# One layer of attention and matmul in float32: steps in batches of two, and softmax denominators summed straight into the heads' rows

## What is computed

```python
q = x @ wq.T + bq;  k = x @ wk.T + bk;  v = x @ wv.T + bv
scores = einsum('bqhd,bkd->bhqk', q, k) / sqrt(32), causal
attn = softmax(scores) @ v
x1 = layernorm(x + attn @ wo.T + bo)
s_x = 448 / max|x1|;  s_w = 448 / max|w|
y = clip(x1 * s_x, -448, 448) @ clip(w * s_w, -448, 448) / (s_x * s_w)
out = layernorm(x1 + y)
```

## Time and profile before

| | us |
|---|---|
| median of 3 runs | 2793.57 |
| lowest, highest | 2790.87, 2796.37 |
| profiled execution, its own time | 2800.54 |
| its span, first to last instruction | 2798.8 |
| PE, DVE, ACT, POOL busy | 2545.9, 1731.8, 1298.5, 728.2 |
| mean granted clock of TensorE | 0.944 of full |

### The profile page before, as it was taken

How to read it: one execution, slowest core, us unless ns; L and a number is a source line. 1 busy time by engine, 2 the same in 40 slices (tenths; PEclk the granted TensorE clock), 3 DMA queues, 4 the chain that set the end, 5 groups by cost and what they waited for, 6 DMA issues and landing times.

```text
span 2798.8 us, 36168 instructions
## 1 busy us (share of the span) xinstructions
PE 2545.9 (91%) x14312; PEld 1553.7 (56%) x14312; DVE 1731.8 (62%) x1293; ACT 1298.5 (46%) x1412; POOL 728.2 (26%) x442
## 2 busy tenths in 40 slices
PE   7999998999999889999989999899999897599998
PEld 5888884344444444444444444444444445488887
DVE  6343438977766666666667767666667764344444
ACT  1222225765665555565655666556656552100000
POOL 2321301221111212121221221212121212466663
PEclk9999998999999999999989999999999999799999
DMA  7343343521221112121121221112121110322221
GB/s 233 114 164 120 114 139 110 125 61 39 50 58 39 39 46 50 39 58 39 39 46 39 50 58 39 40 45 50 39 58 39 39 42 23 128 90 90 90 89 61
DMA packets 150742, 198.01 MB, mean 71 GB/s; under 512 B 8558, under 2 KB 108878, under 8 KB 148558
## 3 DMA queue, kind: packets, MB, share of 16 engines
q1 hardware_dynamic: 126990, 144.71, 19.9%
q10 hardware_dynamic: 23616, 51.39, 4.8%
HBM read 123.72 MB, written 72.35 MB: 70 GB/s over the span
## 4 chain that ended last, share of the span: by engine, by line
PE 80%; DVE 6%; POOL 5%; issue 4%; ACT 2%; DMA 1%; SPq 0%; POOLq 0%; ACTq 0%; DVEq 0%
PE bank L1146 17%; PE bank L1158 17%; PE bank L1131 15%; PE bank L1043 13%; PE bank L1208 13%; POOL moments L521 2%; POOL moments L519 2%; PE bank L1176 2%; ACT prob L697 2%; PE bank L1168 2%; DVE acc L930 2%; DVE stats L751 1%; PE bank L1128 1%; PE bank L1197 1%; DVE res L909 1%
## 5 line engine op out<-in xcount | busy, mean ns | idle before, releaser
L697 ACT ACTIVATE prob<-bank 128x1024 f32<-128x1024 f32 x1088 | 1054.0, 1021 | 554.0 <-PE bank L1146 553.1
L930 DVE TENSOR_TENSOR acc<-acc,prob 128x2048 f32<-128x2048 f32 x420 | 965.0, 2298 | 286.7 <-ACT prob L697 273.8
L1146 PE MATMUL bank<-q_st,keys 98*128 98x512 f32 x2176 | 662.3, 422 | 171.0 <-ACT prob L697 159.4
L1146 PEld LDWEIGHTS bank<-q_st,keys 98*128 98x128 f32 x2176 | 399.5, 196 | 416.5 <-ACT prob L697 325.4
L1158 PE MATMUL bank<-prob,v_t 128*32 128x512 f32 x4352 | 605.1, 629 | 6.6 <-issue 3.4
L568 POOL TENSOR_SCALAR_AFFINE_SELECT prob<-prob 128x1024 f32<-128x1024 f32 x128 | 159.3, 1269 | 996.3 <-ACT prob L697 996.3
L926 DVE TENSOR_TENSOR acc<-prob 128x2048 f32<-128x2048 f32 x60 | 137.5, 2292 | 184.6 <-ACT prob L697 175.8
L1043 PE MATMUL bank<-xt_hi,w_hi 128*128 128x512 f32 x576 | 228.4, 397 | 16.4 <-DVE xt_lo L772 15.7
L1043 PE MATMUL bank<-xt_hi,w_lo 128*128 128x512 f32 x576 | 227.1, 394 | 0.0
L1043 PE MATMUL bank<-xt_lo,w_hi 128*128 128x512 f32 x576 | 226.9, 394 | 0.0
L1131 PE MATMUL bank<-wo_hi,att_lo 128*128 128x512 f32 x512 | 218.6, 427 | 0.0
(11 more groups left out here) (109 smaller groups left out, 2540.8 us busy)
## 6 DMA issues: line engine op xcount, KB each, us to landing
q_st<-q_hi_d SPq DMA_DIRECT2D x128, 256.0 KB
xt_raw<-x_t SPq DMA_DIRECT2D x16, 1024.0 KB, 6.9
q_hi_d<-part_hi ACTq DMA_DIRECT2D x64, 256.0 KB, 2.1
q_lo_d<-part_lo ACTq DMA_DIRECT2D x64, 256.0 KB, 2.3
q_st<-q_lo_d SPq DMA_DIRECT2D x64, 256.0 KB
res<-x SPq DMA_DIRECT2D x32, 512.0 KB, 6.1
x_d<-res SPq DMA_DIRECT2D x32, 512.0 KB, 2.6
x<-x_d SPq DMA_DIRECT2D x32, 512.0 KB, 3.2
```

The costliest lines, as they stand in the source:

```text
L697: nc.scalar.activation(prob[:, s % SLOTS, 2 * p:2 * p + 2], bank[:, 2 * p:2 * p + 2], ACT.Exp, scale=SCALE).then_inc(p_done, 1)
L930: nc.vector.tensor_tensor(acc[:, n % 2], acc[:, n % 2], new, ALU.add).then_inc(acc_done, 1)
L1146: last = nc.tensor.matmul(bank[:, g].rearrange("p (a n) -> p a n", n=P), keys[:, k // QT, k % QT * P:(k % QT + 1) * P], queries[:, :, g], ...
```

## The change

It does five things.

- PE's loop goes by batches `u` of two steps: `scores(2u)`, then `between(u)` (denominators and fillers), `scores(2u+1)`, `weigh_values(2u-2)`, `weigh_values(2u-1)`.
- The denominators are summed by 4 matmuls of 128x512 with a 32-column weight of ones, each into its head's 32 rows. The 4 spreading matmuls of each group are gone.
- VectorE inverts 128x512 instead of 128x128, and multiplies by `r_den` in SBUF instead of a bank in PSUM.
- `places` has new numbers and a tenth name: DEVIATION, where GpSimd does its three small instructions. For the first tile of most pairs: SPLIT 4, HALF0 6 to 12, SUM0 12, HALF1 14 to 20, SUM1 20, DEVIATION 22, SCALE_ROW 27, LARGEST 28.
- The semaphore `ln1` is counted by the moments alone; two new ones, `scaled` and `measured`, count L716 and L951.

```diff
         for n in range(len(groups)):
-            at = begins[n] + lengths[n] + 1
-            den_at.append(max(at, den_at[-1] + 4) if n else at)
+            at = (begins[n] + lengths[n] + 2) // 2
+            den_at.append(max(at, den_at[-1] + 2) if n else at)
...
             if p < len(pairs) - 2:
-                names = (21, 24, 29, 30, 32, 37, 38, 40, 42) if second else (4, 7, 12, 13, 15, 20, 21, 23, 25)
+                names = (21, 24, 30, 30, 32, 38, 38, 39, 44, 45) if second else (4, 6, 12, 12, 14, 20, 20, 22, 27, 28)
...
-        SPLIT, HALF0, HALF0_END, SUM0, HALF1, HALF1_END, SUM1, SCALE_ROW, LARGEST = range(9)
+        SPLIT, HALF0, HALF0_END, SUM0, HALF1, HALF1_END, SUM1, DEVIATION, SCALE_ROW, LARGEST = range(10)
...
-                for place in range(first, last + 1):
-                    fillers.setdefault(place, []).append((q, half, place - first, last - first + 1))
+                for place in range(first // 2, last // 2 + 1):
+                    fillers.setdefault(place, []).append((q, half, place - first // 2, (last - first) // 2 + 1))
...
-                if s in sum1_at:
-                    q = sum1_at[s]
+                if s in deviation_at:
+                    q = deviation_at[s]
                     inverse_deviation(moments[:, q % 2], ln1, q * LN)
                     shift_of(moments[:, q % 2], ln1, q * LN)
...
-                if s - 2 in group_of_end:
-                    n = group_of_end[s - 2]
+                for n in moved_at.get(s, []):
...
-                nc.vector.reciprocal(r_den[:], bank[:, DEN_BANK, 0:P]).then_inc(den_read, 1)
+                nc.vector.reciprocal(r_den[:], bank[:, DEN_BANK]).then_inc(den_read, 1)
...
-                dve.wait_ge(spread_done, n + 1)
+                dve.wait_ge(den_read, n + 1)
                 dve.wait_ge(pv_moved, n + 3)
-                nc.vector.tensor_tensor(attended(n), attended(n), bank[:, DEN_BANK], ALU.mult).then_inc(att_ready, 1)
+                nc.vector.tensor_tensor(attended(n), attended(n), r_den[:], ALU.mult).then_inc(att_ready, 1)
...
-                if s - 1 in group_of_den:
-                    invert(group_of_den[s - 1])
-                if s - 3 in group_of_den:
-                    normalise_group(group_of_den[s - 3])
+                if s % 2 == 0 and s // 2 in group_of_den:
+                    invert(group_of_den[s // 2])
+                if s % 2 == 1 and s // 2 in group_of_den:
+                    normalise_group(group_of_den[s // 2])
...
                 for g in range(HG):
-                    for c in range(QT):
-                        last = nc.tensor.matmul(bank[c * HD:(c + 1) * HD, DEN_BANK, 0:P], head_col[:, g], acc[:, n % 2, g, c * P:(c + 1) * P],
-                                                start=(g == 0), stop=(g == HG - 1), skip_group_check=True)
+                    last = nc.tensor.matmul(bank[g * HD:(g + 1) * HD, DEN_BANK], ones[:], acc[:, n % 2, g], start=True, stop=True, skip_group_check=True)
                 last.then_inc(den_done, 1)
 
-            def spread_out(n):
-
-                pe.wait_ge(den_read, n + 1)
-                for c in range(QT):
-                    last = nc.tensor.matmul(bank[:, DEN_BANK, c * P:(c + 1) * P], spread[:, c], r_den[:], start=True, stop=True)
-                last.then_inc(spread_done, 1)
-
-            for s in range(-1, STEPS + SLOTS_OVER):
-                if s + 1 < STEPS:
-                    scores(s + 1)
-                if 1 <= s <= STEPS:
-                    weigh_values(s - 1)
-                if s in group_of_den:
-                    denominators(group_of_den[s])
-                if s - 3 in group_of_den:
-                    spread_out(group_of_den[s - 3])
-                for q, half, part, parts in fillers.get(s, []):
+            def between(u):
+
+                if u in group_of_den:
+                    denominators(group_of_den[u])
+                for q, half, part, parts in fillers.get(u, []):
                     half_projection(q, half, part, parts)
+
+            for u in range(BATCHES):
+                scores(2 * u)
+                between(u)
+                scores(2 * u + 1)
+                if u >= 1:
+                    weigh_values(2 * u - 2)
+                    weigh_values(2 * u - 1)
+            weigh_values(STEPS - 2)
+            weigh_values(STEPS - 1)
+            for u in range(BATCHES, BATCHES + BATCHES_OVER):
+                between(u)
```

More of the change, by code:

```diff
@@ L66, in build @@
     FIXED = 4 + HG
-    LN = 8
+    LN = 6
     LN2 = 6
@@ L225, in build @@
         den_read = sem("den_read")
-        spread_done = sem("spread_done")
         pv_moved = sem("pv_moved")
@@ L234, in build @@
         ln1 = sem("ln1")
+        scaled = sem("scaled")
+        measured = sem("measured")
         x1_sent = [sem("x1_sent0"), sem("x1_sent1")]
@@ L268, in build @@
         STEPS = len(steps)
-        SLOTS_OVER = 14
+        BATCHES = STEPS // 2
+        BATCHES_OVER = 5
+        SLOTS_OVER = 2 * BATCHES_OVER
         den_at = []
         for n in range(len(groups)):
-            at = begins[n] + lengths[n] + 1
-            den_at.append(max(at, den_at[-1] + 4) if n else at)
+            at = (begins[n] + lengths[n] + 2) // 2
+            den_at.append(max(at, den_at[-1] + 2) if n else at)
         group_of_den = {at: n for n, at in enumerate(den_at)}
-        group_of_end = {begins[n] + lengths[n] - 1: n for n in range(len(groups))}
+        moved_at = {}
+        for n in range(len(groups)):
+            moved_at.setdefault((begins[n] + lengths[n] - 1) // 2 * 2 + 3, []).append(n)
         last_group = {q: n for n, (q, u) in enumerate(groups)}
@@ L284, in places @@
             if p < len(pairs) - 2:
-                names = (21, 24, 29, 30, 32, 37, 38, 40, 42) if second else (4, 7, 12, 13, 15, 20, 21, 23, 25)
+                names = (21, 24, 30, 30, 32, 38, 38, 39, 44, 45) if second else (4, 6, 12, 12, 14, 20, 20, 22, 27, 28)
                 base = (p + 1) * PAIR
             elif p == len(pairs) - 2:
-                names = (17, 20, 23, 24, 26, 29, 30, 32, 33) if second else (4, 7, 10, 11, 13, 16, 17, 19, 20)
+                names = (17, 20, 24, 24, 26, 30, 30, 31, 34, 35) if second else (4, 6, 10, 10, 12, 16, 16, 18, 22, 23)
                 base = (p + 1) * PAIR
             else:
-                names = (39, 40, 40, 41, 40, 40, 41, 42, 43) if second else (30, 33, 34, 35, 36, 37, 38, 39, 40)
+                names = (39, 40, 40, 40, 40, 40, 40, 40, 41, 42) if second else (31, 34, 34, 34, 36, 36, 36, 37, 40, 41)
                 base = p * PAIR
@@ L297, in at_place @@
             return {places(q)[name]: q for q in range(TILES)}
-        SPLIT, HALF0, HALF0_END, SUM0, HALF1, HALF1_END, SUM1, SCALE_ROW, LARGEST = range(9)
-        split_at, sum0_at, sum1_at = at_place(SPLIT), at_place(SUM0), at_place(SUM1)
+        SPLIT, HALF0, HALF0_END, SUM0, HALF1, HALF1_END, SUM1, DEVIATION, SCALE_ROW, LARGEST = range(10)
+        split_at, sum0_at, sum1_at, deviation_at = at_place(SPLIT), at_place(SUM0), at_place(SUM1), at_place(DEVIATION)
         scale_at, largest_at = at_place(SCALE_ROW), at_place(LARGEST)
@@ L561, in _ @@
             nc.gpsimd.memset(share[:].bitcast(F32), 2.0 / P).then_inc(fixed, 1)
+            nc.gpsimd.memset(ones[:], 1.0).then_inc(fixed, 1)
             for s in range(STEPS + SLOTS_OVER):
@@ L714, in _ @@
                     q = scale_at[s]
-                    act.wait_ge(ln1, q * LN + LN - 2)
-                    nc.scalar.activation(res[:, q % 2], res[:, q % 2], ACT.Identity, bias=moments[:, q % 2, 3:4], scale=moments[:, q % 2, 2:3]).then_inc(ln1, 1)
+                    act.wait_ge(ln1, q * LN + LN)
+                    nc.scalar.activation(res[:, q % 2], res[:, q % 2], ACT.Identity, bias=moments[:, q % 2, 3:4], scale=moments[:, q % 2, 2:3]).then_inc(scaled, 1)
             act.wait_ge(y_done, 2 * TILES)
```

22 lines of the change are left out of this document (12 added, 10 removed).

## The result

The changed kernel takes **2603.32 us** (median of 4 runs, 2595.31 to 2610.16), the kernel before 2794.97 beside it (2790.87 to 2800.56). The ratio is 0.931, with an interval of 0.928 to 0.934: 192 us less. The prediction was 2580, with a range of 2450 to 2700 and a chance of 0.94 for faster. Time and sign came out as forecast. What the prediction did not see is found only by the experiments: one of the three parts of the change (the places; the others are the batches and the wide denominators) brings more than the whole.

What follows compares the result with a forecast made beforehand. VectorE was to bound the changed kernel: 98.6 us work, 3 idle and 2.8 clock loss make 104.4 a pair, 1670 for 16; the stage loses 216 us, giving median 2580 us, range 2450 to 2700.

Steps and rivals of the forecast that it cites:

- What bounded before, and the places: Middle stage: PE's work plus stalls before the scaling at L716; later scaling removes the stalls, -15.6 us a pair.
- PE's work: PE per pair of tiles: 102 us before the change, 94 us after with batches, wide denominators and no spread.
- The reciprocal: VectorE's 128x512 reciprocal takes 3.33 us instead of 951 ns: +2.4 us, four times a pair.
- The rival of 4.27 us: Reciprocal at eight cycles an element: 3.8 us more a pair, 2640 us; 0.05 of the first case's chance.
- VectorE's sum: VectorE's additions, reciprocals, multiplies, residuals, moments, largest values and clips: 98.6 us a pair, against 89 before.
- 4 multiplies 3.0 (from SBUF now; taken as before): VectorE's four multiplies by the inverse denominators per pair: 3.0 us, unchanged although now read from SBUF.
- VectorE, not PE, now has the longest work of a pair: After the change VectorE's work per pair exceeds PE's by 4.6 us, 98.6 against 94.
- Lock-step (rival B): PE's waits at SUM0, denominators and cut add up, each dropping the clock: 113 to 118 us a pair, 2717 to 2795; chance 0.13.
- only after 6 us: Argument against more clock falls: the trace before shows one fall per stall, after PE stood 6.00 us.
- Scaling late (C): GpSimd's small instructions wait for VectorE, so ScalarE's wait before scaling returns: 121 us a pair, 2850 us; chance 0.04.
- the change not doing what it says (D): Stall time is set by something else and reappears whole on PE: 2670 to 2800 us; chance 0.03.
- The tail: After the last step the multiply stands behind a 3.3 us reciprocal and the previous tile's moments: +2 us.

Runs made afterwards that it cites:

- The fastest kernel: Changed kernel with narrow denominators, 128x128 reciprocal and spread put back, and denominators of consecutive groups three batches apart instead of two: 2527.62 us, ratio 0.903.
- the kernel with the quarter of a reciprocal: Changed kernel with reciprocals kept in PSUM, but inverting only the first 128 of 512 columns, which the multiply reads four times: 2487.73 us, ratio 0.890.
- Single steps: Kernel before with late scaling, four wide denominator matmuls, 128x512 reciprocal and no spread, one step at a time without batches: 2554.28 us, ratio 0.913.

## Why the prediction was right

**What bounded before, and the places: right.** 15.6 us a pair of stalls was 250 us; the places alone brought 231, and PE was then full at full clock. ScalarE's wait is gone outside the tail.

**PE's work: right.** 102 us a pair stands against 103.5 in the kernel with nothing but the places, of which 0.7 are waits and 0.6 the clock. For batches the terms give 102 - 17 x (2 x 2.12 - 3.90) = 96.2 with narrow denominators. The fastest kernel takes 101.0, of which waits in the stage for other engines (before L1155, L1185, L1137 and L1177) are 34 us or 2.2 a pair, and half clock in 27 us of it costs 0.9: 97.9, 1.7 above the terms. With wide denominators the kernel with the quarter of a reciprocal, with 50 us of waits and half clock in 17 us, leaves 98.4 - 3.1 - 0.5 = 94.8 for the 94 forecast. Two weighings in a row took 1.92 us, wide denominators 1.07, as taken.

**The reciprocal: right.** 3351 ns for 3330. The line through 128x1 and 128x128 holds to 512: (3351 - 951)/384 = 6.25 ns an element. The rival of 4.27 us fell. The Trainium skill (VectorE: DVE Perf Modes, section "Walkthrough: the 8-slice pipeline in each mode") gives the reciprocal's divide a repeat count of 8. Read as eight cycles an element at the page's clock of 0.96 GHz, which is the prediction's reading and not the page's, that would be an estimate of 8.3 ns; the trace disagrees with it.

**VectorE's sum: one term mis-sized.** The step "4 multiplies 3.0 (from SBUF now; taken as before)" failed. The mean was 1114 ns for the 686 of before, 27 us in all or 1.7 a pair; the median is still 685. In the timeline above, GpSimd's subtract of 128x1024 began at 1085.88 and ended at 1088.32, and the multiply, begun at 1086.01, ended at 1088.88, 0.56 us behind it: it went on when GpSimd was through. The Trainium skill (SBUF — State Buffer, section "SBUF: two separate sides") says that a VectorE instruction with two SBUF inputs and a GpSimd instruction that reads SBUF take a shared pair of ports by an exclusive lock, and that the one that starts second stands for the whole instruction of the other. The traces agree: 2873 ns at most with both operands in SBUF, 689 with one in PSUM. The prediction did not weigh that the edit takes the multiply's operand out of PSUM, and should have.

**"VectorE, not PE, now has the longest work of a pair": right as a sum, too strong as a bound.** The sum of 98.6 was about met: VectorE is busy 1493 of 1684 us, or 93.3 a pair, to which come some 3 us for the 0.1 us between the additions in a row, which the sum counts and the busy time doesn't, and what falls into the tail. (The share is 89%, where over 90 was forecast.) But it wasn't what the stage came to. Single steps run the same instructions with VectorE at 96% of the 200 us and a pair in 102.8. The changed kernel's time is made of PE's 94 us and its waits: 73.3 + 27.6 + 16.9 for the three kinds above and 1.4 for the cut make 119 us, the half clock some 50 (a mean of 0.97 is half clock for 6% of 1684 us, half of that lost), and 16 x 94 + 119 + 50 = 1673 for 1684. The forecast of 104.4 reached nearly the same by VectorE's sum, its idle time and one fall of the clock: 98.6 + 3 + 2.8. Its losses were of the right kind, since VectorE runs behind at some batch ends and idles at others, and those of the clock of the right size (2.8 us a pair were forecast, about 3.2 found). But part of this agreement is luck: the sum was counted for VectorE, where the losses fall on PE, 7.4 us a pair of waits for the 3 that were counted as VectorE's idle time.

**What is left of the 23 us.** The median came 23 us above 2580. The stage is 14 of them (1684.4 for 1670). Outside it the profiled execution took 2593.6 - 1684.4 = 909.2 us for the 2798.8 - 1886 + 2 = 914.8 of the sum. And the step from the profiled execution to the median, -7 in the sum because that of before stood above its median, was +8 here, which is 15 more. That term is scatter between executions and could not be forecast.

**Lock-step (rival B): its mechanism is there, its price isn't.** PE does wait at the residual and the denominators, as it had it, though hardly for the cut (1.4 us in the stage), these waits do add up, and the clock does fall after less than 6 us (3.19 above). The kernel before shows that too, against the prediction's "only after 6 us": after a wait of 3.76 us at 1641.29 its window of 1642 to 1646 has a granted clock of 0.64. But they come on top of PE's 94 us and not of VectorE's 98.6, and where one is taken away a part comes back at the others: 23 of 53 us in the kernel with half 1 a batch later.

**Scaling late (C), and the change not doing what it says (D): no.** The last of GpSimd's three small instructions, L534, did get longer, to a mean of 1709 ns for 631 before, but the seven steps from the moments to the scaling hold that. The tail: +2 us was forecast, and from the end of the last weighing to the start of the last scaling it took 37.0 us (2136.5 to 2173.5), 37.4 before (2340.9 to 2378.3).

**What the prediction did not ask** is whether each part pays on top of the others. It priced the wide denominators and the batches against PE's work (-3.6 +0.8, and -8 or so), which is where their gain was, while the price (+2.4 us on VectorE four times a pair) was let into the sum as a new bound. With the places alone the same working gives PE's 102 us a pair and no lag: 2798.8 - 1886 + 16 x 102 + 1.7 is 2546.5, less 7 for the profiled execution 2540, 27 below the 2567 measured and 40 below its own forecast for the whole. That comparison stood ready and was not made.

## What to carry to other kernels

Price each part of a change also on top of the others, not only against the kernel before: here one part alone was worth 231 us, the other two gained 47 before it and cost 36 after it. As these runs have it, work that is moved from a full engine to one with room costs little only while the receiving engine's longest stretch fits between two places that wait for it; its share of busy time (89%) says little. That batches do harm here because they bring such places closer together is how the runs fit together; no run tests it by itself. When you loosen one place of waiting, follow where the time goes: of 53 us here 23 moved on to other waits, and 20 were the price of the edit itself. Less work upstream reached all the places at once (a quarter of the reciprocal: -110 us).

## What the runs showed of the hardware

- A multiply of 128x512 with both operands in SBUF took 0.68 us by itself, 2.86 to 2.87 each time that GpSimd's subtract ran beside it (11 times) and 1.57 beside GpSimd's mask (4 times); with one operand in PSUM never over 0.69. In batches, freeing it passed 20 of its 28 us on to the additions, and the total moved by less than its interval. In single steps it did not, and 16 us were won.
- The reciprocal's time is linear in the elements of a partition at the three sizes seen, 1, 128 and 512: 6.20 ns each to 128 and 6.25 from there to 512. From PSUM to PSUM it is nearly the same (3359 ns) as to SBUF (3351).
- GpSimd's last 128x1 instruction of the chain takes 1709 ns in the mean (L534), 631 before (L526), while the two ahead of it in the attention stage stay near theirs (1904 and 2077 ns for 1896 and 1935). With the places alone it takes 1798 (L528), so it comes with the late scaling and not with batches or wide denominators; why, no run shows.
- PE's granted clock fell from 2.4 to 1.2 GHz after far shorter stalls than the 6.00 us of the earlier trace rows: after 3.19 us above, and here, where PE stood 0.73 and 0.18 us. Timeline and window of the changed kernel:

```profile
1033.33 1.19 PE L1154 MATMUL bank<-q_st,keys 98*128 98x512 f32 x4
...
1035.25 0.74 PE L1154 MATMUL bank<-q_st,keys 98*128 98x512 f32 x2 [0.73 <-ACT prob L706]
...
1036.17 0.80 PE L1154 MATMUL bank<-q_st,keys 98*128 98x512 f32 x2 [0.18 <-ACT prob L706]
...
1036.90 3.49 PE L1166 MATMUL bank<-prob,v_t 128*32 128x512 f32 x16
...
1036.00:1040.00 4.00, 3.83 (x18) 0.89 (x18) 3.75 (x5) 2.05 (x3) 3.58 (x3) 0.59 0.00 0
```

Two weighings take 3.49 us there for 1.92 at full clock, at a granted clock of 0.59. The same wait of about 0.73 us stands 15 times in the changed kernel behind the first pair of tiles, and the clock fell right behind it at four of them. What made it fall there and not at the others was not tried, and stays open.
